# Four attentions of a transformer tower: output products, a layer norm, gate logits, value pieces and a band mask are put elsewhere in the order of the engines

## The reference

```python
h = tok(x)
h = h + L0_attn(ln(h))       # heads of 16, rotary, causal mask
h = h + L0_ffn(ln(h))        # 8 experts
h = h + L1_attn(ln(h))       # a grid attention
h = h + L1_ffn(ln(h))        # attention: heads of 64, q and k normalised, gated heads
h = h + L2_attn(ln(h))       # attention: heads of 64, a second layer norm with gamma, beta
h = h + L2_ffn(ln(h))        # 8 experts, top 2
h = h + L3_attn(ln(h))       # heads of 16, scores + band, band = (|i-j| <= 32)
h = h + L3_ffn(ln(h))        # 16 experts, top 8
# each attention: softmax(q k^T * scale + mask) v, then @ Wo + bo
```

## Time and profile before

| | us |
|---|---|
| median of 3 runs | 732.2 (731.81, 732.2, 741.64) |
| the profiled execution's own time | 738.21 |
| its span, first to last instruction | 736.5 |
| TensorE busy | 696.1 (95%) |
| VectorE busy | 500.9 (68%) |
| ScalarE busy | 351.5 (48%) |
| mean granted TensorE clock, share of full | 0.963 |

### The profile page before, as it was taken

How to read it: one execution, slowest core, us unless ns; L and a number is a source line. 1 busy time by engine, 2 the same in 40 slices (tenths; PEclk the granted TensorE clock), 3 DMA queues, 4 the chain that set the end, 5 groups by cost and what they waited for, 6 DMA issues and landing times.

```text
span 736.5 us, 16233 instructions
## 1 busy us (share of the span) xinstructions
PE 696.1 (95%) x6345; PEld 629.9 (86%) x6345; DVE 500.9 (68%) x1240; ACT 351.5 (48%) x809; POOL 167.1 (23%) x164
## 2 busy tenths in 40 slices
PE   6999999999999999999998999999999999999996
PEld 6788898999988777798877998889999967779995
DVE  3658468888877952878565783577766768556785
ACT  0367355555543232678443442455544445247663
POOL 1200026544351122334022000035443220000000
PEclk9999899999999998999798998999999999699999
DMA  9922022222221000002200010022231200112100
GB/s 250 270 69 81 2 58 79 80 80 79 65 68 58 1 0 1 3 2 74 58 1 1 2 45 2 31 73 60 71 107 28 85 1 2 52 42 80 32 23 24
DMA packets 16283, 39.40 MB, mean 54 GB/s; under 512 B 3596, under 2 KB 4588, under 8 KB 15759
## 3 DMA queue, kind: packets, MB, share of 16 engines
q1 hardware_dynamic: 14232, 37.29, 17.7%
q10 hardware_dynamic: 1976, 1.08, 0.6%
HBM read 37.90 MB, written 0.44 MB: 52 GB/s over the span
## 4 chain that ended last, share of the span: by engine, by line
PE 74%; DVE 15%; issue 4%; ACT 4%; POOL 2%; DMA 1%; POOLq 0%; ACTq 0%; DVEq 0%; SPq 0%
PE PS L720 7%; PE PS L849 6%; PE PS L793 5%; PE PS L601 4%; PE PS L605 4%; PE PS L603 4%; PE PS L604 4%; PE PS L602 4%; PE PS L729 4%; PE PS L814 3%; PE PS L653 3%; DVE AL L1571 2%; PE PS L839 2%; PE PS L656 2%; PE PS L655 2%
## 5 line engine op out<-in xcount | busy, mean ns | idle before, releaser
L1034 ACT ACTIVATE MIX<-PS 128x288 f32<-128x288 f32 x118 | 48.4, 411 | 116.7 <-PE PS L605 116.4
L601 PE MATMUL PS<-XH,WH 128*128 128x288 f32 x284 | 86.7, 305 | 3.4 <-DVE OT L1560 1.4
L1893 POOL TENSOR_TENSOR rstd<-var,nhalf 96x3 f32<-96x3 f32 x18 | 17.9, 992 | 295.3 <-DVE var L1307 295.3
L603 PE MATMUL PS<-XH,WL 128*128 128x288 f32 x284 | 83.9, 295 | 0.0
L602 PE MATMUL PS<-XL,WH 128*128 128x288 f32 x284 | 83.8, 295 | 0.0
L604 PE MATMUL PS<-X,WH 128*128 128x288 f32 x284 | 83.7, 295 | 0.0
L605 PE MATMUL PS<-X,WL 128*128 128x288 f32 x284 | 83.6, 294 | 0.0
L1560 DVE TENSOR_TENSOR OT<-MIX,PS 128x288 f32<-128x288 f32 x94 | 42.2, 450 | 39.0 <-ACT MIX L1034 38.4
L1571 DVE TENSOR_TENSOR AL<-OT,AH 128x288 fp32r<-128x288 f32 x118 | 58.9, 507 | 3.3 <-ACT AH L1048 2.3
L1414 DVE TENSOR_TENSOR WL<-RG,WH 128x768 fp32r<-128x768 f32 (+2 forms) x46 | 57.8, 1258 | 3.5 <-ACT WH L1014 3.3
L653 PE MATMUL PS<-AH,DW 128*128 128x288 f32 x166 | 52.3, 315 | 7.2 <-DVE AL L1571 7.0
(11 more groups left out here) (256 smaller groups left out, 1737.8 us busy)
## 6 DMA issues: line engine op xcount, KB each, us to landing
RG<-in_gu_l0f_dram SPq DMA_DIRECT2D x8, 512.0 KB, 4.5
RG<-in_gu_l0f_dram SPq DMA_DIRECT2D x16, 256.0 KB, 5.7
RG<-in_gu_l2f_dram SPq DMA_DIRECT2D x9, 384.0 KB, 3.6
RG<-in_gu_l2f_dram SPq DMA_DIRECT2D x18, 192.0 KB, 4.3
RD<-in_wd_l0f_dram SPq DMA_DIRECT2D x8, 384.0 KB, 3.2
RD<-in_wd_l2f_dram SPq DMA_DIRECT2D x9, 288.0 KB, 2.8
RD<-in_wd_l3f_dram SPq DMA_DIRECT2D x6, 384.0 KB, 3.1
BIG<-in_patch_dram SPq DMA_DIRECT2D x6, 288.0 KB, 8.3
```

The lines of the kernel that those rows point to most:

```text
L601: mm(o, WH[r][:, 0, w], XH[:, cols], start=True, stop=False)
L603: mm(o, WL[r][:, 0, w], XH[:, cols], start=False, stop=False)
```

## The change

**The three tiles of the first half's output.** In A1 and A2 (`wide`) tile 0, 1 and 2 go one each into three passes: tile 0 into the pass that held nothing of it before in A1 (one pass sooner), tile 2 into the pass after, ahead of that pass's `scores`. In A0 and A3 all three go together, behind the last `scores` and ahead of that pass's `turn_probs` and `mix`. The parts of the next stage's layer norm follow: one pass sooner in A0, A1 and A3.

**A1.** The gate logits are cut into four groups of two pairs of sequences, one behind each of the value pieces 4 to 7. ScalarE's exponential of the gates moves to pass 1. The split of A2's weights moves out of A1's tail into its passes: ScalarE at the ends of passes 8, 9, 11, 13, 15 and 16, VectorE at 9, 10, 12 and 16, the last two pieces in A2's passes 0 and 1. The load of these weights is cut into three, and the parts start as A1 has done with what they overwrite.

**A2.** The second half's layer norm no longer stands ahead of the first unit: part 0 stands at the top of VectorE's pass 0, part 1 at the end of pass 1, part 2 at the end of pass 2; `turn(stage, 1)` is in TensorE's pass 3, and the copies out of it in pass 4. The second half's value pieces go into passes 5, 6 and 7, in banks 2 and 3. The first `mix` waits for the second half's copies, as they share its banks.

**A3.** The band mask is added by TensorE ahead of the scores, as in A0; VectorE's sum is gone. The query copies are VectorE's as before.

```diff
 def pieces(a, i):
     n = 4 if a.tm else 3
+    i -= 4 if a is A2 else 0
...
+def value_bank(a, j, p):
+    return (2 if a is A2 and j else 4 + 2 * j) + p % 2
...
-W2 = [(0, 1536, 2304), (1, 1536, 2304), (0, 0, 768), (1, 0, 768), (0, 768, 1536), (1, 768, 1536)]
+W2 = [(0, 1536, 2304), (1, 1536, 2304), (1, 0, 768), (0, 0, 768), (0, 768, 1536), (1, 768, 1536)]
...
# SyncE
-            sp.wait_ge(S["tm_ready"], TM0["l1f"] + A1.units)
-            qkv(A2)
+            second_weights(0, A2.v0, A2.width)
+            for n in range(2):
+                sp.wait_ge(S["tm_ready"], TM0["l1f"] + 9 + 3 * n)
+                second_weights(1 + n, 768 * n, 768 * (n + 1))
...
# TensorE, attention()
+                            if u == 0 and k == 0:
+                                pe.wait_ge(S["y_taken"], TAKEN[stage])
...
-                    masked = a is A0
+                    masked = a.paired
...
+                    if u == (a.ng if a is A2 else 0):
+                        pe.wait_ge(S["v_sb"], V0[a.name] + 2 * a.vpieces)
                     if u == 0:
-                        pe.wait_ge(S["v_sb"], V0[a.name] + 2 * a.vpieces)
+                        wait_xv(a, 1)
...
-                            if a.gated and p == 6:
-                                gate_logits()
                             values(0, p)
+                            if a.gated and p >= 4:
+                                last = gate_logits((2 * p - 8, 2 * p - 7))
+                                if p == 7:
+                                    last.then_inc(S["logits"], 1)
+                    if a is A2 and i == 3:
+                        turn(stage, 1)
                     for p in pieces(a, i):
                         values(1, p)
                     if 0 <= i - lag < a.units:
                         qk(i - lag)
+                    n = i - lag - a.units
+                    if wide and n == 0:
+                        output(range(2, TAU), range(a.ng)).then_inc(S["y_ready"], 1)
                     if 0 <= i - lag - 1 < a.units:
                         scores(i - lag - 1)
+                    if n == (-2 if wide else 0):
...
+                        last = output(range(1 if wide else TAU), range(a.ng))
+                        if not wide:
+                            last.then_inc(S["y_ready"], 1)
+                    if wide and n == -1:
+                        output(range(1, 2), range(a.ng))
...
-                        output(range(1), range(a.ng))
-                    if i == a.first_out + 1:
-                        output(range(1, TAU), range(a.ng)).then_inc(S["y_ready"], 1)
# ScalarE, attention()
-                    if a is A1 and i >= a.units + lag + 1:
-                        for n in range(2):
-                            w2_split(2 * (i - a.units - lag - 1) + n)
+                    if a is A1 and i in (8, 9, 11, 13, 15, 16):
+                        w2_split((8, 9, 11, 13, 15, 16).index(i))
# VectorE
-                for part in range(3):
-                    layer_norm(k, 1, (part,))
-                    if a is A2 and part < 2:
-                        w2_split(2 + part)
+                if a is A2:
+                    return
+                layer_norm(k, 1)
...
-                    if a.mask and a is not A0:
-                        mk = masks[:, 0 if a.mask == "causal" else 1, :]
-                        link(V.tensor_tensor(e, s, mk.unsqueeze(1).to_broadcast([a.rows, HB, N]), ALU.add))
-                        s = e
...
+                    if a is A2 and i == 0:
+                        layer_norm(stage, 1, (0,))
+                    if a is A2 and i == 4:
+                        evac_xt(stage, "attn", a, 1)
...
+                    tail = wide and i >= a.units + lag
+                    if tail and 0 <= i - lag - 2 < a.units:
+                        norm(i - lag - 2)
+                    part = i - lag - a.units - (0 if wide else 1)
+                    if wide and 0 <= part < 3:
+                        if a is A1 and part == 2:
+                            w2_split(3)
+                        layer_norm(stage + 1, 0, (part,))
...
+                    if a is A2 and i in (1, 2):
+                        layer_norm(stage, 1, (i,))
+                    if a is A2 and i < 2:
+                        w2_split(4 + i)
```

79 lines of the change are left out of this document (39 added, 40 removed).

## The result

| | before | after |
|---|---|---|
| median of 20 runs each, us | 737.9 (731.74 to 743.93) | 732.7 (730.16 to 738.4) |
| the profiled execution's own time | 738.21 | 732.45 |
| its span | 736.5 | 730.7 |
| mean granted TensorE clock | 0.963 | 0.981 |

The ratio is 0.9942 with a 95% interval from 0.9916 to 0.9968: the changed kernel is 4.3 us faster, between 2.4 and 6.2 (the two medians are 5.2 apart). That is clear of the noise, but under half of the 11.2 us of the forecast's sum, and the time is 6.7 us above the forecast of 726. The median of 732.2 that stands ahead of the prediction came from three runs; over 20 runs the kernel before takes 737.9, which is where its profiled execution stood. The ratios in this document leave out three executions of the experiments' sessions that stood far above the others of their kernel (1627.0 of the kernel before, 954.7 of e6, 730.8 of e3).

The account below looks back on a forecast made before the run. TensorE, busy 95% of the span, was taken as the bound, through its work, waits and clock. Terms of -0.7, -3.4, -4.7, +5.1, -3.5 and -4.0 gave -11.2: 738.2 to 727.0 us; 726 was taken, range 717 to 735.

Parts of the forecast that it names:

- the price of the tails (-4.7 and -3.5): Ends of A1 and A2: shorter waits (-1.3, -1.2) and less low clock (-3.4, -2.3) save 4.7 and 3.5 us.
- the price of A2's start (+5.1): Start of A2: the new order loses 5.1 us, +2.6 by waits and value pieces and +2.5 by clock.
- after a wait of 5.8 I expect the low level for about 5 us of work: Start of A2: low clock behind TensorE's wait for VectorE ahead of the second half's transposes costs +2.5 us.
- the second rival: Start of A2: clock stays low for about 14 us of work instead of 5, total 733 us; chance 0.15.
- 37.8 against 35.3: Start of A2: pass 5's start, new (with 7.2 us of value pieces still to come) against before; gives +2.6 us.
- VectorE's chain ... with one `shift` and one `norm` now inside it: A1's tail: VectorE's layer norm chain, 8.9 us before, takes about 9.4; TensorE's 1.78 wait shrinks to 0.5.
- The gates: A1: cutting the gate logits in four removes the 6.8 us low-clock stretch behind them, saving 3.4 us.
- A3: A3: mask on TensorE and sooner output save 4.9 us if the low clock goes, 0.9 held back: -4.0.
- A0: End of A0: layer norm about 1 us sooner, the 0.72 wait goes, -0.7 us; clock left out.
- A1's weight splits: A1's passes: extra copies on ScalarE and VectorE cost 0; 1.2 us in all if their cover were gone.
- The base of the whole: Whole kernel: sum made against the profiled 738.2, not the median 732.2; 727.0 either way, or 721.0 otherwise; 726 taken.
- what was to show it: Signs: gate window at 1.00; in A2 a 6 us wait, VectorE idle 7, `turn_probs` idle gone; A3 passes at 3.6.

Follow-up runs that it names:

- e9: The changed kernel with 36 dead products ahead of A2's second-half transposes and 10 more ahead of the first `mix`, filling both TensorE waits; 728.8 us.
- e5: The changed kernel with 36 dead products in TensorE's 5.23 us wait ahead of A2's second-half transposes; 729.6 us.
- e2: The changed kernel with the start of A2 put back as it was before, all else as changed; 723.0 us.
- e12: The changed kernel with the output tiles and layer norm of A1's and A2's tails as before; 734.5 us.
- e10: e8 with TensorE's scores of the last unit ahead of the third output tile in A1 and A2; 716.1 us.
- e6: The changed kernel with A1's 16 small gate-logit products back in one run ahead of value piece 6; 734.4 us.
- e3: The changed kernel with A2's second-half layer norm at the top of VectorE's pass 0, its transposes and copies in pass 1; 721.8 us.
- e7: The changed kernel with A3's band mask added by VectorE again, output tiles as changed; 735.1 us.
- e1: The kernel before with only A3's edits: mask on TensorE, output tiles together, layer norm a pass sooner; 734.6 us.
- e8: The changed kernel with the edits of e3 and e4 together; 720.1 us.
- e4: The changed kernel with VectorE's `shift` of the last unit ahead of the next layer norm's first part, in A1 and A2; 728.9 us.

## Why the prediction came out as it did

Two steps of the prediction failed: the price of the tails (-4.7 and -3.5), which is the larger miss, and the clock and the base in the price of A2's start (+5.1).

**A2, the start: a step that failed, by its clock and above all by its base.** The waits were right to a few tenths. With T = 0 at 374.16 the second `qk` starts at 10.7 (10.6 was forecast), the transposes at 21.2 (21.4), the waits are 1.04 and 5.23 (1.1 and 5.8); and in e9, where the level stays at 1.00, pass 5 begins at T = 30.8, where 30.6 was forecast ahead of the clock's price. What failed is "after a wait of 5.8 I expect the low level for about 5 us of work": the stretch held 11.7 us of work, nearly to the first `mix`, and pass 5 began at T = 34.2. The length was far off, the price less so, 3.4 us for 2.5, because the slower TensorE no longer met the wait for the first `mix` (1.4 forecast, 1.36 in e5, none here). That is the second rival, "the hole in A2 is deeper" (the paragraph on the skill calls it the third). The reason I gave against it, that `qk` alone had kept the full level in the middle of A2, did not hold behind a hole: passes 3 and 4 there are `qk`, `scores` and `turn_probs`, and stayed at 0.50. With the hole filled (e5, e9) the same passes are at 1.00. But that the rival's 733 is nearly the time measured is luck: it put 7 us more into A2, and A2 missed by 2.9; the rest of the distance lies in A1 and in A0's start.

The base, "37.8 against 35.3", failed by more: the term was counted against a start with 10.2 us of low clock in it, which is not there behind A1's new tail. In e2 the old start's pass 5 begins at 404.04, T = 32.5. e2 shows the price: 10.1 us in A2 and 9.7 in the medians, where the sum had +5.1. Of the 5.0 us between, 0.8 are clock (3.3 in e9 for 2.5) and 4.2 the rest (6.8 for 2.6): 2.8 of them the base, and 1.0 TensorE's two waits for VS (0.58 and 0.41) behind pass 5, which the sum did not look at. Against the kernel before as its profile stood, the start cost 4.5 + 1.9 (e12's tail) = 6.4 us, 1.3 more than forecast.

**The tails: the largest miss.** The forecast was -4.7 for A1's and -3.5 for A2's, 8.2 together; e12 gives 2.7 and 1.9 by the profiles (0.8 for A1 by the other five), 1.8 by the medians. The wait before A1's transposes went, as forecast (none instead of 0.5), and the stretch of 10.2 became 3.4 in this profile and twice 3.4 in six others. The step that failed is "VectorE's chain ... with one `shift` and one `norm` now inside it": it asked when the chain would end and not who waits for the `shift` inside it. That was ScalarE and, behind its copy of PT, TensorE: 2.19 us, more than the 1.3 that the tail was to save in waits. In A2 the same order left 1.07 of the 1.24 that were to go. With both waits for PT gone, in e10, A1 is 97.4 - 93.1 = 4.3 us under e12's, close to the 4.7 forecast, and A2 is 2.5 under e3's. So the idea of the tail was right and the `shift` was what it lacked.

**The gates: right.** The window is at 1.00, and e6 gives 3.3 us by the profiles for the 3.4 forecast.

**A3: right.** M3's first transposes stand 42.97 us behind those of A3's second half, where the forecast was 43.0 with all the clock back and 43.9 with the 0.9 held back: -5.0 for -4.0. The passes take 3.5 us, the wait of 1.71 for ES is gone.

**A0: the place where only the wait was counted.** It gave 2.8 us for 0.7, 2.7 of it in the clock behind the tail, which I had left out of the sum though the tail got the same edit as A3's. The wait of 0.72 for XN itself went, but the late products, whose cover the tiles had been, wait 0.50 for OT.

**A1's weight splits: right at nothing.** From `token_major`'s start to TensorE's wait for QB at the end of these passes it is 348.34 - 266.73 = 81.6 us before and 345.93 - 267.67 = 78.3 after, and the difference is the gates' 3.3.

**The base of the whole.** The sum was made against 738.2 and gave 727.0, and I argued that the median of 732.2 would lead to about the same. The 20 runs put the base at 737.9, so three runs had been lucky and nothing had to be reconciled. By the two profiles the sum failed like this: A2 and A1 cost 4.8 us more than forecast, A0's tail and A3 3.1 less, and 3.8 by the start of A0 and the loading are in no term: -11.2 + 4.8 - 3.1 + 3.8 = -5.7 for the -5.8 measured. The 3.1 are in part luck: the clock behind A0's tail was in no term of the sum.

**By what was to show it:** the gate window at 1.00, the wait of about 6 in A2, VectorE's idle 7 us and A3's rows came; the idle ahead of the late `turn_probs` of A2 did not go (1.24 to 1.07), it changed its cause from PN to PT.

The Trainium skill ("TensorE: Matmul & The Clock Gate", section HAM oscillation) says that idle gaps between bursts throttle the clock; e9 agrees, as filling two gaps took the whole stretch away. The stretch behind the gate logits (e6), which stands behind no gap, is not told by it. Part 4 of the page says that transposes do not count as busy work for it; in e9 they ran at 1.00 in a row of filled passes, so here that had no price by itself.

## What to carry to other kernels

When a step is moved on an in-order engine, ask of every instruction that it now stands ahead of who waits for that one, and follow the answer through the next queue: here part 0 of a layer norm held a `shift`, the `shift` held an exponential, and the exponential held the copy that TensorE wanted. A chain that can run in an idle stretch belongs ahead of the first instruction that waits, as e3 shows with 10 us. And where the clock pays most of a change, look at how far the passes behind a wait are thin, as the low level lasted through all of them here (11.7 us of work); do not price a tail's clock from one profile, as the next one can have a stretch more; and do not take low stretches of the old profile as belonging to the place where they stand: an edit further ahead can remove them.

## What was not expected of the hardware

A wait does not always bring the low level, and its length alone does not say: 1.83 us in e2 left the clock at 1.00, 1.71 in e7 and 1.36 in e5 had 6.8 us at 0.50 behind or around them, 2.33 in the kernel before had 6.8 and the same wait in e1, 2.11, had 3.4. Nor does the low level need a wait: the one behind the gates (e6) has none ahead of it, and the one of 3.4 us in A1's tail in e10 has none above 0.52. Stretches in identical code come and go between kernels: in the start of A0 it is 6.8 us in the changed kernel and in e8, 3.4 in e1, e7 and e9, and none in the kernel before, e2 to e6 and e10 to e12; in M3 one of 3.4 us (1.6 us of time) is in ten of the twelve experiments, but not in the kernel before, the changed one, e4 and e6. In A0's start it goes with the loading: the five profiles with a stretch are those in which the first transposes start at 21.75 us or later, and in the nine without they start at 21.55 or sooner. Why a few tenths should matter is not shown, and what decides it elsewhere stays open. It is also why the kernel before spreads over 12 us: beside the experiments its runs at a mean clock of 0.956 took 741 to 744 us, those at 0.967 to 0.972 took 732 to 736.
